# One query and key projection per batch in the first attention, its high and low parts laid out per unit through scratch memory

## The reference, cut to what matters

```
k_eff = (W_dq.T @ W_uq.T @ W_uk).reshape(nh, hs, n_kvl)      # nh = 16 heads of hs = 8
c_kv = x @ W_dkv.T
q = (x @ W_dq.T @ W_uq.T).reshape(B, T, nh, hs)
q_lat = einsum('bqhd,hdl->bhql', q, k_eff)
attn = softmax(causal(einsum('bhql,bkl->bhqk', q_lat, c_kv) / sqrt(hs)))
y_lat = einsum('bhqk,bkl->bhql', attn, c_kv)
y = einsum('bhql,hld->bqhd', y_lat, v_eff).reshape(B, T, C)
```

## Time and profile before

| | us |
|---|---|
| runs of the kernel before | 1148.64, 1136.71, 1145.32 |
| their median | 1145.32 |
| profiled execution: span from first to last instruction | 1156.0 |

### The profile page before, as it was taken

One profiled execution on the slowest core, in us unless ns is written; L12 is line 12 of the kernel. 1 busy time (PEld: TensorE's weight loads), 2 busy tenths in 40 slices (PEclk: granted clock), 3 DMA queues, 4 the chain that ended last, 5 costly groups with the idle time before them and its releaser, 6 DMA issues.

```text
span 1156.0 us, 17351 instructions
## 1 busy us (share of the span) xinstructions
PE 918.9 (79%) x5550; PEld 659.8 (57%) x5550; DVE 751.8 (65%) x1959; ACT 567.5 (49%) x1139; POOL 446.8 (39%) x374
## 2 busy tenths in 40 slices
PE   3899988799999989699999778990288767979920
PEld 3566666444444444566668558980166545769920
DVE  4677755667777763667774686883478972858832
ACT  3566653155555554656665547870121122748810
POOL 2355520100000000355552675517388840765345
PEclk9999998699999995699998889995599965969965
DMA  5022310000000002012213016861011211067822
GB/s 150 1 74 74 89 66 1 1 3 3 2 1 1 1 2 74 1 37 74 73 37 92 28 61 207 281 207 51 24 8 19 29 11 46 1 193 266 275 64 68
DMA packets 102721, 77.90 MB, mean 67 GB/s; under 512 B 40721, under 2 KB 79295, under 8 KB 102655
## 3 DMA queue, kind: packets, MB, share of 16 engines
q1 hardware_dynamic: 97662, 66.85, 18.6%
q0 software_dynamic: 4992, 10.23, 3.8%
HBM read 35.11 MB, written 10.22 MB: 39 GB/s over the span
## 4 chain that ended last, share of the span: by engine, by line
PE 50%; DVE 21%; issue 12%; ACT 8%; POOL 5%; DMA 2%; another core or an unknown queue 1%; DVEq 1%; SPq 1%; POOLq 0%
PE banks L1949 6%; DVE normed L1212 5%; ACT hid_high L905 5%; PE banks L1632 5%; PE banks L1634 4%; PE banks L1633 4%; POOL y_rows L791 4%; PE banks L1987 4%; PE banks L2081 3%; PE banks L1925 3%; PE banks L1751 2%; PE banks L1967 2%; DVE wide L1221 2%; PE banks L1975 2%; DVE banks L1433 2%
## 5 line engine op out<-in xcount | busy, mean ns | idle before, releaser
L1433 DVE CUSTOM_DVE_ANT_0 banks<-banks,consts 128x384 f32<-128x384 f32 (+3 forms) x256 | 122.8, 510 | 57.9 <-PE banks L1949 53.7
L1003 ACT ACTIVATE wide<-banks 128x1024 f32<-128x1024 f32 (+3 forms) x128 | 90.0, 705 | 102.8 <-PE banks L1975 101.1
L1215 DVE TENSOR_TENSOR hid_low<-normed,hid_high 120x512 fp32r<-120x512 f32 x96 | 93.1, 970 | 67.0 <-ACT hid_high L905 67.0
L779 POOL DMA_INDIRECT x_rows<-xn_d,idx_u x92 | 89.1, 968 | 65.2 <-PE banks L1858 37.2
L905 ACT ACTIVATE hid_high<-normed 120x512 fp32r<-120x512 f32 x96 | 60.7, 632 | 89.3 <-DVE normed L1212 89.1
L1321 DVE TENSOR_TENSOR hid_low<-hid_full,hid_high 128x256 fp32r<-128x256 f32 x184 | 76.1, 425 | 28.9 <-issue 12.2
L1949 PE MATMUL banks<-aarena 32*128 32x384 f32 (+3 forms) x256 | 87.5, 392 | 6.4 <-DVE mx L1433 5.7
L791 POOL DMA_INDIRECT y_rows<-y_d,pos_u x64 | 60.5, 946 | 68.1 <-DMA y_d<-y_turned 49.2
L1623 PE MATMUL banks<-consts,normed 128*128 128x128 f32 x96 | 23.0, 408 | 79.6 <-DVE normed L1126 66.9
L1632 PE MATMUL banks<-ei_high,w_high 128*120 (+1 forms) x192 | 80.6, 420 | 4.7 <-ACT ei_low L863 2.4
L721 POOL TENSOR_TENSOR wide<-eo 128x2048 f32<-128x2048 f32 x16 | 72.0, 4498 | 11.6 <-ACT eo L1051 11.6
(11 more groups left out here) (283 smaller groups left out, 2672.8 us busy)
## 6 DMA issues: line engine op xcount, KB each, us to landing
warena<-in_L_ffn_w_kernel SPq DMA_DIRECT2D x32, 344.0 KB, 3.3
spare_uh<-u_high SPq DMA_DIRECT2D x30, 256.0 KB
spare_ul<-u_low SPq DMA_DIRECT2D x30, 256.0 KB
spare_dh<-d_high SPq DMA_DIRECT2D x30, 256.0 KB
spare_dl<-d_low SPq DMA_DIRECT2D x30, 256.0 KB
y_d<-y_turned SPq DMA_DIRECT2D x46, 128.0 KB
warena<-in_L_ffn_wo_kernel SPq DMA_DIRECT2D x16, 300.0 KB
u<-in_L_ffn_We SPq DMA_DIRECT2D x1, 2048.0 KB
```

The costliest lines, as they stand in the source:

```text
L1003: act.activation(pt[:, kt, 2 * rp:2 * rp + 2, q0:SEQ], pairs[1 + rp][:, :, q0:SEQ], ACT.Exp, scale=SCALE).then_inc(s["exp"], 1)
L1215: dve.tensor_tensor(hid0_l[0:m, ring, :], hid0_f[0:m, ring, :], hid0_h[0:m, ring, :].bitcast(F32), ALU.subtract).then_inc(mx0["rest"], 1)
L1433: ins = dve.tensor_tensor_reduce(part, part, CAUSAL[:, SEQ - n:SEQ], 1.0, NEG, ALU.add, ALU.max, mx[:, j % 2, qt, r:r + 1])
```

## The change

The projection is done once for all 16 heads of a batch with plain weights of 128 x 128 (`wq_n`, `wk_n`): eight in all instead of 32. ACT's `hi` and DVE's `low` write the high and the low part of the whole batch into a staging tile `qk_st`. SP stores them to a scratch tensor `qk_d` in the chip's memory, three stores of 256 KB per projection (one of the parts stands twice), and loads each unit's queries and keys from it as two loads of 256 KB in the row order of `qs` and `ks`. The fourth group of 8 rows of each head is written once, as zeros for queries and two rows of ones for keys: eight stores of 256 KB from `u1` before We1 is loaded into it.

The projections of batches 0 and 1 come first, those of batches 2 and 3 in steps 1, 2 and 5, 6 at x = 0. The value projection comes before the maxima of unit 0. PE waits for a unit's loads before its maxima (`heads_landed`), at the head of the step. The loop is now twice four steps, and steps 9 to 12 are written out. The uses of bank 6 are renumbered.

```diff
+UNIT_USES = [6, 9, 12, 14]
+PER_BATCH = 10
-        wq_rep = sb("wq_rep", [P, NH, 4, HD])
-        wk_rep = sb("wk_rep", [P, NH, 4, HD])
+        wq_n = sb("wq_n", [C, C])
+        wk_n = sb("wk_n", [C, C])
...
-        qk_hi = aarena[:, 8 * SEQ:10 * SEQ].rearrange("p (k q) -> p k q", k=2)
+        qk_st = over("qk_staged", "ei", 0, [P, 2, 2, 2, SEQ], F32R)
+        qk_ones = u1[:, 0:2, :]
+        qk_d = nc.dram_tensor("qk_d", (BATCH, 2, NH, 4, HD, SEQ), F32).ap()
...
+            def rows_of_ones():
+                sp.wait_ge(zeros_up, 2)
+                for k in range(2):
+                    for b in range(BATCH):
+                        sp.dma_start(qk_d[b, k, :, 3, :, :], qk_ones[:, k, :]).then_inc(ones_out, 16)
+            def heads(s):
+                def parts_out(n, b, k):
+                    sp.wait_ge(s["a_free"], n + 1)
+                    for part in range(3):
+                        low = part == 1 + k
+                        dst = qk_d[bass.ds(b, 1), k, :, part, :, :].rearrange("b h d q -> (b h) d q")
+                        sp.dma_start(dst, qk_st[:, b_parity(b), k, int(low), :].bitcast(F32)).then_inc(s["qk_out"], 16)
...
+                def unit_in(b, j):
+                    for k, dst in enumerate((qs, ks)):
+                        src = qk_d[bass.ds(b, 1), k, 4 * j:4 * j + 4, :, :, :].rearrange("b h p d q -> (b h p d) q")
+                        sp.dma_start(dst[j].bitcast(F32), src).then_inc(s[f"qk_in{j % 2}"], 16)
+                def maxima_in(u, j):
+                    sp.wait_ge(s["nm"], u + 1)
...
+                def step(u, b, j, out=None):
+                    sp.wait_ge(s["st"], 8 * u)
+                    if j == 1:
+                        sp.wait_ge(s["qk_out"], 96 * (b + 1))
+                    unit_in(b, (j + 3) % 4)
+                    if out is not None:
+                        parts_out(*out)
+                    maxima_in(u + 1, (j + 1) % 4)
+                for n in range(2):
+                    parts_out(n, 0, n)
+                sp.wait_ge(ones_out, 32 * BATCH)
+                sp.wait_ge(s["qk_out"], 96)
+                for j in range(2):
+                    unit_in(0, j)
+                for n in range(2):
+                    parts_out(2 + n, 1, n)
+                maxima_in(0, 0)
+                unit_in(0, 2)
+                maxima_in(1, 1)
+                unit_in(0, 3)
...
+            rows_of_ones()
+            sp.wait_ge(ones_out, 32 * BATCH)
             sp.dma_start(u1[:, 0:E, :], a[f1 + "We1"].rearrange("e c i -> c e i")).then_inc(f1_in, 16)
             sp.dma_start(u1[:, E, :], a[f1 + "Ws1"]).then_inc(f1_in, 16)
-            maxima(PH[1])
+            heads(PH[1])
...
+                    act.activation(qk_st[:, b if isinstance(b, int) else 0, k, 0, :], B[projected(n)], ACT.Copy).then_inc(s["a_hi"], 1)
...
-                    dve.scalar_tensor_tensor(dst[j], qk_hi[:, k, :].bitcast(F32), lo, B[projected(n)], ALU.mult, ALU.add)\
+                    dve.tensor_tensor(qk_st[:, half, k, 1, :], B[projected(n)], qk_st[:, half, k, 0, :].bitcast(F32), ALU.subtract)\
...
+                def heads_landed(u, j):
+                    pe.wait_ge(s[f"qk_in{j % 2}"], 32 * (u + 1))
...
+                    if "b" in do:
+                        heads_landed(ahead, j % 2)
                     for x in range(8):
                         scores(u, j, x, (u + 2, (j + 2) % 4, MAX_FIRST[x]) if "b" in do else None)
-                        if x == 0 and "a" in do:
-                            project(n, b + 1 if j else b, (j + 3) % 4, 0)
+                        if x == 0 and part is not None:
+                            project(n, *part)
                             n += 1
...
-                        if x == 4 and "a" in do:
-                            project(n, b + 1 if j else b, (j + 3) % 4, 1)
-                            n += 1
```

More of the change, by code:

```diff
@@ L165, in constants @@
     part("rev")[:] = E - np.arange(E)
[L166 to L169, removed]
+    part("k_one")[:, 0] = np.arange(P) % HD < 2
     return t
@@ L836, in take @@
                 act.wait_ge(prep_ps, k + 1)
[L837 to L841, removed]
+                act.activation(dst, B[k % 2][0:rows, 0:cols], ACT.Copy).then_inc(prep_sb, 1)
             def mixture0(s, first):
@@ L995, in max_hi, with step @@
                     act.activation(nm[:, 0, :], B[6][0:4, :], ACT.Identity, scale=-1.0).then_inc(s["nm_hi"], 1)
[L997 removed]
+                def step(u, j, base, do, part=None):
                     n = base
@@ L1013, in step @@
                             n += 1
-                for n in range(6):
-                    hi(n, n % 2)
-                max_hi(6, 0, 0)
+                for n in range(4):
+                    hi(n, n // 2, n % 2)
                 for q in range(4):
@@ L1453, in heads_add, with step @@
                     dve.tensor_tensor(xs, xs, o4, ALU.add).then_inc(s["heads"], 1)
-                def step(u, b, j, base, do):
+                def step(u, b, j, base, do, part=None):
                     n = base
@@ L1461, in step @@
                             heads_add(n - 1, u - 1, b if j else b - 1, (j + 3) % 4)
-                        if x in (1, 5) and "a" in do:
-                            split(n, u + 3, (j + 3) % 4, x // 4)
+                        if x == 1 and part is not None:
+                            low(n, *part)
                             n += 1
@@ L1990, in weigh, with step @@
                         ins.then_inc(s["pv"], 1)
-                def step(u, b, j, base, do):
+                def step(u, j, base, do, ahead=None, part=None):
                     n = base
@@ L2018, in step @@
                             weigh(u, j, *WEIGH[x - 3])
-                for n in range(6):
-                    project(n, 0, n // 2, n % 2)
-                pe.wait_ge(s["a_free"], 2)
-                for g in range(NMAX):
-                    rows(0, 0, g)
-                max_rows(6, 0, 0)
+                for n in range(4):
+                    project(n, n // 2, n % 2)
                 for t in range(TILES):
+                    if t % 4 == 0:
+                        pe.wait_ge(s["a_free"], t // 4 + 1)
                     ins = pe.matmul(B[2 + t // 4][:, P * (t % 4):P * (t % 4) + P], xt_tile(t), wv[:, :],
@@ L2030, in attention @@
                         ins.then_inc(s["v_ps"], 1)
+                heads_landed(0, 0)
+                for g in range(NMAX):
+                    rows(0, 0, g)
+                max_rows(4, 0, 0)
+                heads_landed(0, 1)
                 for g in range(NMAX):
```

131 lines of the change are left out of this document (68 added, 63 removed).

## The result

The changed kernel takes 1226.0 us (median of four runs, 1218.64 to 1229.56), the kernel before, in the same session, 1144.46 (four runs, 1136.71 to 1148.64): a ratio of 1.0715 [1.066, 1.0771]. It was forecast faster at 1120. It is 7% slower. A ratio in this text counts only executions within 1.5% of the fastest of their kernel, and the brackets are its 95% interval.

A forecast was written before the change was run, and what follows sets the result against it. PE alone was taken to be full in the first attention, at clock 1.00. The terms -27.8 + 2.4 + 0.5 = -24.9 us gave 1131.1 off the profiled 1156.0, 1120 off the median; range 1110 to 1135.

The forecast's parts named there:

- the price of a step without projections: First attention loop: each step would take 11.19 us like step 13 of before, instead of 13.72, saving 2.53 us.
- rival 3: Loop: without the long full-row projections the clock falls to 0.50, +5.9 us a step, 1191 us; chance 0.07.
- The loop, removed and added: Loop: projections removed give -30.4 and -2.5 us, four put back at 1.27 us each cost 5.1; sum -27.8 us.
- rival 2: Loop: late per-step transfers make every step wait 1.2 us for rows or negated maxima; 1135 us; chance 0.08.
- The stall of step 1: Head of step 1: PE waits for loads queued behind unit 1's maxima; 0.5 us, bounds 0 and 2.5.
- Before the loop: Stretch ahead of step 0: round trip through memory delays first maxima 6.8 us, step 0 by 2.4 (bounds 0.6 and 6.3).
- Rival 1: Round trip at its dear end: prologue +6.3 us and a 2.5 us stall in step 1; 1126 us; chance 0.19.
- The rule that I weighed: Skill's rule that matmul loops repeatedly waiting for DMA are slowed; judged to add nothing for the wait before unit 0.

The follow-up runs named there:

- e3: Kernel before, no scratch memory or new DMA, with the projections of steps 1 to 12 computing 32 columns instead of 512; 1239.83 us.
- g1: Kernel before plus fillers in steps 14 and 15 alone (one dense matmul a sub-step, 22 in step 14's wait); 1155.69 us, ratio 0.9925.
- e2: Changed kernel plus two unused float32 128x128x512 matmuls in each of steps 0 to 12 where the change took projections out; 1177.31 us.
- e9: The kernel of e2 again, word for word, over ten executions; median 1177.21 us, ratio to before 1.0038.
- e5: Changed kernel plus eight unused bfloat16 128x128x512 matmuls a step, in steps 0 to 13; 1141.25 us.
- h1: Changed kernel plus four dense bfloat16 matmuls a step (x = 0 to 3), also in steps 14 and 15, and 22 in step 14's wait; 1136.99 us, ratio 0.9834.
- e8: e5 with its eight matmuls a step in steps 14 and 15 too, and 22 in the wait of step 14; 1133.30 us.
- e10: The kernel of e8 again, over ten executions; median 1152.57 us, ratio to before 0.9899.
- h2: e8 with six dense matmuls a step instead of eight, all at x = 0 to 3 (two at x = 1 and 2); 1143.82 us, ratio 0.9877.
- f1: e8 plus full-row matmuls in the stretch before the loop, and 20 of the 24 warming matmuls taken away; 1289.87 us, ratio 1.1116.
- e1: Changed kernel plus two unused float32 128x128x512 matmuls in step 0 alone; 1240.70 us.
- e4: Kernel before with only step 0's two projections narrowed to 32 columns; 1284.68 us.
- h3: Changed kernel plus four dense bfloat16 matmuls a step at x = 0, 2, 4, 6 in steps 0 to 13, ten executions; 1148.70 us, ratio 0.9915.

## Why the prediction was wrong

**The step that failed** is the price of a step without projections. The forecast took it from step 13 of before, 11.19 us at 1.00 ("That is the experiment the change makes, already in the trace"), for every step of the loop, and the last sentence of rival 3 used the same step against the fall of the clock: "Against: step 13 ran 11.2 us without projections at 1.00." I read one step of before as proof of thirteen. Measured, such a step took 18.73 us at 0.50. Step 13 is entered at full clock from twelve steps with projections, and it lasts one step. In after the first such step, step 0, lost the clock 3.4 us behind its mark, and in `e3` step 1, entered at full clock from a step with both projections like step 13, lost it some 4 us behind its mark (247.55).

Nor is step 13 itself safe: of the four profiles in which it is entered at full clock without filler, before and `g1` kept the clock in it and `e2` and `e9` lost it 2.4 and 2.6 us behind its mark. So the step that the forecast was built on need not have kept its clock either. The latter two have the change and the former two haven't, so whether chance or the kernel made the difference is open; with the DMA share at 0.00 around the fall in `e2`, traffic of the moment didn't.

The mechanism of rival 3 was named right ("the projections are the only long matmuls over all 128 rows in a step"), and it got 0.07. `e3` shows the fall without the change's DMAs, and `e5` and `h1` show the clock held with all of them. That it is the rows of these matmuls, and not another trait of them, is argued and not shown (see the end).

**The size of rival 3.** It said 17.1 us a step and 1191. Measured: 18.73, 1.67 times 11.19, where I took 1.53 from the durations of one pair of matmuls. Such durations overlap (at 237.94 and 237.95 two begin together), and the period is what counts. The sum with what was measured: nine steps lose 18.73 - 11.19 = 7.54 us, four with a projection 21.03 - 12.5 = 8.53, step 0 14.61 - 10.2 = 4.4: 67.9 + 34.1 + 4.4 = 106.4. Rival 3 had twelve steps of 5.9, 71. Added to the forecast of 1120 it is 1226.4, against 1226.0 measured. Part of that closeness is luck: the terms before the loop were 2.3 us too dear (below), and the forecast set one execution against a median, with a scatter of 11 us.

**The loop, removed and added**, holds where the clock does, as far as kernels with fillers show it; none ran the loop without them at 1.00. `e5` has 12.75 us with eight fillers, `h1` 11.90 with four: 0.21 a filler, which leaves 11.05 for none (step 13 of before: 11.19). A projection adds 1.26 in `e5` and 1.24 in `h1` (forecast 1.27). So the 27.8 us of the loop are borne out, and the clock takes nearly four times as much (106.4).

**DMAs of the step** (rival 2): no wait in any step of after. At full clock `e5`, `e8` and `e10` have none either, so this isn't owed to the longer steps alone. The stall of step 1 that I put at 0.5 us is 0.75 in `h1`, 0.5 in `h2` and 0 in `e5` and in after, whose steps are longer. It didn't lower the clock in `h1`.

**Before the loop** I forecast 2.4 us and measured 0.56. The first maxima came 5.3 us later instead of 6.8, but not because the round trip was cheaper. The stores began at 196.99 and not at 199.1, as the stage had started earlier in this execution; from the first store to the first maxima it is 11.0 us, where I had 10.4 (199.1 to 209.5). The stores were issued one in 0.69 us (six in 4.13), not in 0.5:

```profile
196.99 4.13 SPq L541 DMA_DIRECT2D qk_d<-qk_staged  x6
204.53 1.76 SPq L550 DMA_DIRECT2D aarena<-qk_d  x4
```

The last store goes out at 201.1 and the loads 3.4 us behind it. While the stores drain, the DMA engines are nearly full, at the rate that I had taken (300 GB/s):

```profile
199.00:203.50 4.50, 4.35 (x34) 3.73 (x32) 1.38 (x2) 3.06 (x6) 0.00 (x0) 1.00 0.93 301
```

Rival 1 (the dear round trip) is out. The Trainium skill's 207 GB/s for rows far apart ("DMA: Bandwidth & Descriptors", "Latency and other measured facts") is no ceiling for heads 64 KiB apart: the stores moved 301 here.

**The range** left rival 3 out at 0.07, and the chance was the mistake: the trace of before held a case of a lost clock that full work didn't bring back (431 to 458), and a single step against it.

**The rule that I weighed.** In the loop PE was busy throughout where the clock fell in after, in `e2` and in `e3`. The Trainium skill, "TensorE: Matmul & The Clock Gate", section "HAM oscillation — how this bites in real kernels", ties the loss of the clock to waits for DMA in a matmul loop. By that rule alone, which I weighed ahead of the result, after's loop with no DMA wait in it should have stayed at 1.00; the trace says 0.51, and the measurement decides. Where PE did stand idle the traces agree: in after the clock fell at 205.5, within the 4.66 us that PE waited for the loads of unit 0, in before at 428.0, within the 4.80 us ahead of 431.05, and in `f1` some 2 us behind an idle 2.77 us.

## What to carry to other kernels

Before you take long full-row matmuls out of a loop of narrow ones (32 of 128 rows), ask what else in the loop holds PE's clock: at 0.50 the step was 1.67 times as long, and taking out 28 us of work made this stretch 79 us longer. One step at full clock in the trace is no proof for a row of them, and one run near the edge is no proof either way; time such a version ten times. If the clock needs company, matmuls that compute nothing can hold it: four a step (0.2 us each) at x = 0 to 3, with the filling of steps 14 and 15, gave back some 89 us in four of four executions.

## What the runs showed of the hardware

- The granted clock fell with PE busy in all of the time around the fall (after: 239.0 to 240.0; `e3`: 5.00 of 5.00 us, DMA share 0.00). What is left in such a step are matmuls over 32 rows, weightings with 32 result rows and transposes. In `e1`, `e2` and `e9` it fell just inside step 1 all the same, in `e1` while a projection over all 128 rows ran.
- What holds the clock doesn't restore it with certainty: at 0.50, two projections a step in `e4` and eight fillers a step in `f1` left it there for twelve and more steps. In `e2` the same amount of work as in `e4` had it back after two steps (292 us). What tells these two apart is open, and two of the ten executions of `e9`, the same kernel as `e2`, look by time and mean clock like `e4`.
- Amount alone doesn't decide. Two float32 matmuls a step are 2.2 us of full-row work and fell in both profiles of `e2` and `e9`; four in bfloat16 are 0.8 us and held in seven of ten (`h3`) and, at x = 0 to 3, in four of four (`h1`). Spread and place seem to matter; `h1` also has the filling of steps 14 and 15 and only four runs, so its place isn't shown to be the reason.
- The kernel before kept its clock in the loop in its profile and, by their times, in each of its other executions here (1136.71 to 1170.43 us), although its steps carry the same projections as `e2`. It wasn't tried whether `e2` falls for its DMAs on top, or for the order in which its step begins. Nor was it tried whether long fillers over 32 rows would do: that it is the rows and not another trait of these matmuls is argued from the score matmuls, which are 512 columns long themselves and didn't hold it.
- A fall of the clock with PE busy isn't the same in every execution: step 13 without filler, entered at 1.00, stayed at 1.00 in two profiles (before, `g1`) and fell in two (`e2`, `e9`).
- Late in the stage the clock is worth little: `g1`, with 1.00 or nearly (0.98) in 424 to 455 instead of 0.56, is 0.9925 [0.9871, 0.9978] of before. That ratio counts seven of its ten executions; by the medians of all it is 0.995.
